# Second image of a two-image layer: the powers of its two norms, its routing and its counts in other places

## What is computed

```python
x = conv_attention(x)        # group norm, q k v, softmax attention with 4 heads, projection, residual
t = to_tokens(x)
t = t + attn(ln_t(t))        # linear attention: softmax of keys over the tokens, of queries over each head
t = t + ffn(ln_t(t))         # mixture of experts, below
def ffn(x):
    logits = x @ Wr + br;  probs = softmax(logits)      # 8 experts
    top_p, top_idx = top_k(probs, 2);  weights = top_p / top_p.sum()
    xn = (x - mu) * rsqrt(var + 1e-5)
    y_e = gelu((xn * ln_g[e] + ln_b[e]) @ W1[e] + b1[e]) @ W2[e] + b2[e]
    return weights[0] * y_top0 + weights[1] * y_top1
```

## Time and profile before

| | us |
|---|---|
| median of three runs | 360.91 |
| the profiled execution | 360.62 |
| its span, first to last instruction | 358.9 |
| TensorE busy | 315.1 (88%) |
| VectorE busy | 202.1 (56%) |
| ScalarE busy | 194.5 (54%) |
| GpSimd busy | 113.7 (32%) |

### The profile page before, as it was taken

The page is one execution under the profiler, slowest core; times in us unless marked ns, Lnnn a source line. Parts: engine busy times, 40 slices in busy tenths (PEclk is TensorE's granted clock), DMA queues, the critical chain, the costliest instruction groups (busy, mean ns, idle before and its releaser), DMA issues.

```text
span 358.9 us, 6251 instructions
## 1 busy us (share of the span) xinstructions
PE 315.1 (88%) x1885; PEld 197.5 (55%) x1885; DVE 202.1 (56%) x620; ACT 194.5 (54%) x303; POOL 113.7 (32%) x190
## 2 busy tenths in 40 slices
PE   7979898899999989999999878796545599999986
PEld 3533443343444435355443336785444499999985
DVE  2585456475766753465747746766752057776610
ACT  1470676477676754546667320647332277777722
POOL 2073094000000000100031884015277745656630
PEclk9995999899999999999999998897858599999999
DMA  6069785835000007000000112100011422224215
GB/s 197 4 132 207 161 206 234 231 87 211 2 2 3 3 18 219 0 2 1 2 0 0 55 37 61 38 0 22 10 52 52 111 61 63 76 76 132 77 55 211
DMA packets 20540, 27.88 MB, mean 78 GB/s; under 512 B 3831, under 2 KB 14508, under 8 KB 20252
## 3 DMA queue, kind: packets, MB, share of 16 engines
q1 hardware_dynamic: 15800, 17.57, 18.3%
q0 software_dynamic: 3520, 9.39, 8.3%
q10 hardware_dynamic: 1188, 0.53, 0.6%
HBM read 11.15 MB, written 8.33 MB: 54 GB/s over the span
## 4 chain that ended last, share of the span: by engine, by line
PE 63%; issue 11%; POOL 11%; DVE 8%; ACT 3%; DMA 3%; SPq 0%; DVEq 0%; ACTq 0%; POOLq 0%
PE ps L913 14%; POOL expert_in L530 9%; PE ps L1132 8%; PE ps L1112 8%; PE ps L890 8%; PE ps L871 4%; PE ps L855 4%; PE ps L750 2%; PE ps L790 2%; PE ps L822 2%; POOL rstd L466 1%; DMA Qs<-mrow 1%; DVE pm L1247 1%; PE ps L1091 1%; PE ps L1163 1%
## 5 line engine op out<-in xcount | busy, mean ns | idle before, releaser
L598 ACT ACTIVATE probs<-ps 128x1024 f32<-128x1024 f32 x64 | 65.3, 1020 | 35.1 <-PE ps L890 35.0
L913 PE MATMUL ps<-probs,vT 128*32 128x512 f32 x256 | 68.6, 612 | 0.6 <-ACT probs L598 0.5
L913 PE MATMUL ps<-probs,ones 128*32 128x512 f32 x256 | 68.6, 612 | 0.0
L466 POOL TENSOR_TENSOR rstd<-ve,minus_half 128x1 f32<-128x1 f32 (+2 forms) x6 | 10.3, 1724 | 147.4 <-DVE ve L1298 77.3
L1112 PE MATMUL ps<-w,GT 128*128 x312 | 45.9, 294 | 12.0 <-ACT GT L728 11.7
L1244 DVE CUSTOM_DVE_ANT_0 above<-ps,above 128x512 f32<-128x512 f32 x56 | 38.6, 691 | 29.9 <-PE ps L871 27.4
L1112 PEld LDWEIGHTS ps<-w,GT 128*128 128x128 f32 x312 | 41.5, 207 | 13.6 <-issue 13.5
L1132 PE MATMUL ps<-XTT,w1s 128*128 128x128 f32 x312 | 46.2, 296 | 2.9 <-issue 2.7
L536 POOL DMA_INDIRECT token_out<-Y,yidx x39 | 37.7, 966 | 33.4 <-DVE Y L1571 28.7
L890 PE MATMUL ps<-Qs,Ks 98*128 98x512 f32 x128 | 43.6, 421 | 2.3 <-DMA Qs<-mrow 1.6
L1132 PEld LDWEIGHTS ps<-XTT,w1s 128*128 128x128 f32 x312 | 42.6, 211 | 4.3 <-issue 3.9
(11 more groups left out here) (224 smaller groups left out, 440.1 us busy)
## 6 DMA issues: line engine op xcount, KB each, us to landing
XR<-expert_in SPq DMA_DIRECT2D x39, 65.0 KB, 1.9
Qs<-q_hi SPq DMA_DIRECT2D x16, 128.0 KB, 3.1
w<-in_L_ffn_W SPq DMA_DIRECT2D x1, 2048.0 KB, 8.5
w<-in_L_ffn_W SPq DMA_DIRECT2D x8, 256.0 KB, 4.5
YG<-token_out SPq DMA_DIRECT2D x8, 256.0 KB, 3.9
Ks<-k_hi SPq DMA_DIRECT2D x14, 128.0 KB, 2.7
expert_in<-zeros POOLq DMA_DIRECT2D x1, 1300.0 KB, 5.6
expert_in<-zeros POOLq DMA_DIRECT2D x1, 1235.0 KB, 8.1
```

Source lines behind the costliest of these rows:

```text
L598: nc.scalar.activation(probs[:, s % 3, :], bank(2 + 2 * (s % 2), 2), ACT.Exp).then_inc(exp_done, 1)
L913: last = nc.tensor.matmul(bank(value_bank(o))[i * HD:(i + 1) * HD, :], w, probs[:, s % 3, hd * HALF:(hd + 1) * HALF], start=kt == 0, stop= ...
```

## The change

- The tables: for the second image, VectorE runs *route* and *choose* directly behind *shift* (step 2), where they stood behind step 3; the *counts* go from behind step 4 to "3 mid" on VectorE and from "5 mid" to "3 mid" on TensorE; ScalarE runs all of *norm2* behind the exponential of step 2.
- The power of the second norm is one operation for each of its two rows, for both images; the gates wait for the first alone, the shift for both. The other waits count one more.
- The power of the second image's first norm stands ahead of the sixth pair of stores (`J - 3`) and not of the seventh (`J - 2`): behind ten stores, where it stood behind twelve.

```diff
--- before.py
+++ after.py
@@ -311,12 +311,12 @@
                      48: "queryT_sb", 49: "attend stats", 50: "tokenT", 51: "tokenT_sb", 52: "logits shift",
                      53: "gates_exp", 54: "route choose norm2_0", 55: "norm2_1", 56: "norm2_2 counts", 57: "norm2_3"}
         LAYER1_PE = {"before": "residual project query_value0 query_value1 keys", 0: "keyT", "1 mid": "context queryT fold",
-                     1: "attend", "2 mid": "tokenT", 2: "logits", "5 mid": "counts"}
+                     1: "attend", "2 mid": "tokenT", 2: "logits", "3 mid": "counts"}
         LAYER1_DVE = {"before": "tokens_stats tokens query_value0 query_value1 query_max keys",
                       0: "queries queries_scaled", "1 mid": "context fold", 1: "attend stats",
-                      2: "logits shift", 3: "route choose", 4: "counts"}
+                      2: "logits shift route choose", "3 mid": "counts"}
         LAYER1_ACT = {"before": "tokens_stats", "first": "queries_exp keys_exp keyT_sb", "1 mid": "queryT_sb",
-                      "2 mid": "tokenT_sb", 2: "gates_exp", 3: "norm2_0 norm2_1", 4: "norm2_2 norm2_3"}
+                      "2 mid": "tokenT_sb", 2: "gates_exp norm2_0 norm2_1 norm2_2 norm2_3"}
         def run_parts(parts, where, step, b):
 
             for name in where.get(step, "").split():
@@ -463,8 +463,9 @@
                 b, second = (n - B) // 2, (n - B) % 2
                 i, rows, columns = (n, 1, 1) if n < B else (B + 3 * b + second, 1 + second, J)
                 pool.wait_ge(var_ready, n + 1)
-                nc.gpsimd.tensor_tensor(rstd[:, i:i + rows, 0:columns], ve[:, i:i + rows, 0:columns],
-                                        minus_half[:, 0:rows, 0:columns], ALU.pow).then_inc(rstd_ready, 1)
+                for r in range(i, i + rows):
+                    nc.gpsimd.tensor_tensor(rstd[:, r, 0:columns], ve[:, r, 0:columns], minus_half[:, 0, 0:columns],
+                                            ALU.pow).then_inc(rstd_ready, 1)
 
             rsqrt(0)
             rsqrt(1)
@@ -539,7 +540,7 @@
             rsqrt(B)
             rsqrt(B + 1)
 
-            scatter(0, lambda j: rsqrt(B + 2) if j == J - 2 else None)
+            scatter(0, lambda j: rsqrt(B + 2) if j == J - 3 else None)
             rsqrt(B + 3)
             for t in range(SENT_FIRST):
                 send(t)
@@ -1301,7 +1302,7 @@
                 last.then_inc(var_ready, 1)
 
             def norm_apply(src, dst, i, n, done):
-                dve.wait_ge(rstd_ready, n + 1)
+                dve.wait_ge(rstd_ready, n + 1 + (n - B) // 2)
                 for j in range(J):
                     last = nc.vector.tensor_scalar(dst[:, j, :], src[:, j, :], lmv[:, j, 0:1], rstd[:, i, j:j + 1],
                                                    ALU.subtract, ALU.mult)
@@ -1376,7 +1377,7 @@
                 norm_stats(t2[:, b, :, :], B + 3 * b + 1, twice=True)
 
             def v_shift(b):
-                dve.wait_ge(rstd_ready, B + 2 * b + 2)
+                dve.wait_ge(rstd_ready, B + 3 * b + 3)
                 nc.vector.scalar_tensor_tensor(nm2[:, b, :], lmv[:, :, 0], -1.0, rstd[:, B + 3 * b + 2, :], ALU.mult,
                                                ALU.mult).then_inc(nm2_ready, 1)
 
@@ -1385,7 +1386,7 @@
 
             def v_gates(b):
                 dve.wait_ge(lg_ready, b + 1)
-                dve.wait_ge(rstd_ready, B + 2 * b + 2)
+                dve.wait_ge(rstd_ready, B + 3 * b + 2)
                 link(nc.vector.tensor_tensor(lg[:, :, :], ps[:, 0:J * E].rearrange("p (j e) -> p j e", j=J),
                                              rstd[:, B + 3 * b + 1, :].unsqueeze(2).broadcast_to([P, J, E]), ALU.mult))
                 link(nc.vector.tensor_tensor(lg[:, :, :], lg[:, :, :], rb[:, :].unsqueeze(1).broadcast_to([P, J, E]), ALU.add))
```

## The result

The changed kernel takes 364.27 us, median of 14 runs (362.47 to 365.84), against 360.97 for the kernel before, 14 runs: a ratio of 1.0116 [1.0092, 1.0139], so 3.3 us slower. The profiled execution has a span of 362.9 us, before 358.9.

The account below looks back on a forecast made before the run. The chain to the second image's last store on GpSimd was taken as the bound, with a constant time behind it. -0.1 + 4.85 - 0.91 = +3.8 on the profiled 360.62 led to a forecast of 364.6 us, range 362.3 to 366.8.

Parts of the forecast that it names:

- The front: Second image's first power, two stores earlier: ends 2.25 us sooner, but ScalarE's copies leave the chain only 0.1 won.
- The split: Second power as two operations: gates start at 242.26 instead of 243.51, routing 1.9 us sooner.
- The rival of waiting gates: VectorE's second gate operation waits for GpSimd's second power: routing 0.74 us later, 365.3 us; chance 0.07.
- The counts: Counts at tile 3, on TensorE and VectorE: start at 249.5 instead of 253.38, slots 3.9 us sooner.
- The wait for results 2 and 3: GpSimd's sends ahead of the stores wait for results behind VectorE's counts: first store at 263.1 instead of 258.26, 4.85 lost.
- The stores: The sixteen stores on GpSimd keep a steady pace: 18.93 us from first to last start instead of 19.84, 0.91 won.
- The end: Time from the last store's start to the end, thirty tiles on TensorE, taken as constant at 80.8 us.
- The restart: Rival: after the longer wait TensorE's slow clock costs twice the 3.0 us, 367.6 us; chance 0.05.
- The sum of 3.8: Whole chain: front -0.1, wait for sends +4.85, stores -0.91, so 3.8 us slower.
- The rival in which the sends hold nothing back: GpSimd's stores start at the slots, winning the slots' 3.9 and the 0.1: 356.6 us; chance 0.04.

Follow-up runs that it names:

- e5: Kernel before with only the first power moved ahead of two more stores (J - 3): 360.02 us, ratio 1.0037.
- e7: Changed kernel with two sends instead of four ahead of the stores and the first power back behind twelve stores: 356.85 us, ratio 0.9928.
- e11: Kernel before with two unused products filling TensorE's idle time ahead of tile 4's first product: 357.9 us, ratio 0.9945.
- e3: Kernel before with two sends instead of four ahead of the second image's stores: 360.33 us, ratio 1.0013.
- e1: Changed kernel with two sends instead of four ahead of the second image's sixteen stores: 356.5 us, ratio 0.9896.
- e2: Changed kernel with three sends instead of four ahead of the second image's stores: 362.75 us, ratio 1.0057.
- e8: Changed kernel, four sends, with the second image's tile table and affine columns moved on VectorE behind tile 3's result: 358.45 us, ratio 0.9979.
- e9: Changed kernel with two sends ahead of the stores and tile table and affine columns on VectorE behind tile 3's result: 355.18 us, ratio 0.9869.
- e6: Kernel before with only the second power split in two operations, with its wait counts: 358.1 us, ratio 0.9945.

## Why the prediction was right

- **The front, -0.1.** ScalarE's key exponential starts 15.89 behind `ve`, before 16.06, although the power ended 2.25 sooner (210.86 + 1.67 against 212.57 + 1.68, each from its `ve`): the copies of tiles 0 and 1 hold ScalarE back, as said, since the rows of tile 0 are loaded only from 222.34 on, behind the last store of the first image (220.05), and TensorE idles for them (the 4.97 above). e5 and e7 confirm it. The second power came 0.07 sooner. In ScalarE's timeline the copies end at 225.64, and both exponentials follow without a wait:

```profile
224.61 1.03 ACT L707 ACTIVATE XTT<-ps,affine 128x128 f32<-128x128 f32 x2 [13.96 <-PE ps L1092]
...
226.49 1.10 ACT L611 ACTIVATE xn<-ps,kneg 128x1024 f32<-128x1024 f32 x1
```

- **The split, 1.25 at the gates and 1.9 at the routing.** Measured 1.32 and 1.97. The exponential's table load (243.09, 1.28 long) did end last. The rival of waiting gates is out: the operation with both inputs in SBUF ran at 242.98 for 0.23, inside the powers of 240.94 to 244.22.
- **The counts, 3.9.** Measured 3.94 at the copy and 3.94 at the slots. What the prediction did not see is the clock's part in this: TensorE was granted 0.81 of it here before, and the counts of the kernel before were late partly for that (1.36 by e11); in e3 the mask came 1.49 later than before and the counts' copy only 0.12, so it was not the mask that they waited for. The step's size came out right because the prediction built it on the mask and the addition behind it, and the changed kernel's counts do wait for the mask (5.70, above), not for TensorE's groups.
- **The wait for results 2 and 3, +4.85.** Measured +4.58, the front's 0.07 included; from the slots' start to the first store it is 8.97, forecast 9.18. Tile 2's result began before the last affine column was finished, where I had laid one behind the other. The chain, e1 and e2 show that this is the cause, e8 that the table work in front of tile 2's result is its larger part.
- **The stores, -0.91.** Measured 18.94 from first to last, so -0.90. The reason given was near: beside VectorE's table operations stood the first and the third store (1.63 and 1.19 long), not the first two.
- **The end.** The time behind the last store's start stayed (80.59 against 80.80). The restart was no slower for the longer idle time, as this window says beside the earlier trace rows:

```profile
286.50:293.00 6.50, 6.32 (x29) 5.73 (x30) 1.64 (x4) 3.50 (x7) 3.39 (x6) 0.54 0.45 116
```

The sum of 3.8 is 3.47 in the rows behind `ve` and 3.3 in the medians: 364.6 forecast, 364.27 measured. The rival in which the sends hold nothing back had been priced at 356.6; e1, which takes the two sends out of the way, took 356.5.

## What to carry to other kernels

Work that is moved ahead moves other work behind: look at what every in-order queue still has in front of the instruction that is to profit, and at what those entries wait for, before counting the gain. Here a queue's two sends made 7.8 us of difference, and one constant mended it. An idle stretch of TensorE is also worth its clock: two products without use in a hole of 2.45 us brought the kernel before to 0.9945 [0.9924, 0.9966] of its time. It does not always pay: five of them ahead of tile 9 kept the clock, and no gain is shown.

## What the runs showed of the hardware

**An indirect store and some VectorE operations hold each other up.** The 0.91 that the steady stores win has a cause that I had only guessed at. VectorE's timeline of e1 beside its stores above: a comparison and a multiplication, both with two inputs in SBUF.

```profile
252.60 0.91 DVE L1476 TENSOR_TENSOR xn<-t_iota,ends 128x720 f32<-128x720 f32 x1
...
255.87 0.41 DVE L1489 TENSOR_TENSOR xn<-xn,vcol 128x240 f32<-128x240 f32 x1
```

In most cases a store that starts inside such an operation is longer than 0.96, and by just so much as if it had started 0.13 before that operation's end: 252.60 + 0.91 - 0.13 - 252.71 = 0.67 (measured 0.68), and 255.87 + 0.41 - 0.13 - 255.92 = 0.23 (0.23). In e9 a store at 260.38 beside the multiplication of 260.32 took 1.18 by the same sum, and one that had started 0.45 before the comparison was not longer. So what waits seems to lie in the first part of a store. In e6 it went the other way: the store took its usual time, and the multiplication beside it 0.48 instead of 0.41. The first line is VectorE's, the second GpSimd's:

```profile
259.46 0.48 DVE L1489 TENSOR_TENSOR xn<-xn,vcol 128x240 f32<-128x240 f32 x1
```

```profile
259.51 0.95 POOL L531 DMA_INDIRECT expert_in<-X,slots  x1 [0.30 <-issue]
```

The same pair stands in e7 (257.21 and 257.26), and the stores of these two runs take 19.60 and 19.61 from first to last where e1's take 19.88. What decides which of the two waits is not shown: in e1, as in e6, the store started 0.05 behind the multiplication.

The Trainium skill (SBUF — State Buffer, "SBUF: two separate sides") states that VectorE and GpSimd share a pair of ports, and that whichever operation starts first (on VectorE, one in a two-port mode, or one with two SBUF inputs against a GpSimd operation that reads SBUF) holds it for its whole instruction while the other waits. It also states that GpSimd cannot write a transfer's descriptors while VectorE runs an operation in a two-port mode. The stores agree, with the sums above, in that one of the two waits beside an operation with two SBUF inputs; in e6 and e7 it was the multiplication, although it started first. The power does not: beside two powers of 3.28 together, VectorE's operation with two SBUF inputs took its usual 0.23.

**The power's cost** grows with its elements: 8 took 1.67, 16 took 2.93, two of 8 together 3.28. Splitting cost 0.35 of GpSimd and gave the first result 1.25 sooner.
